# Attention and mixture of experts on one core: where the shared expert's tiles stand among the attention slots, and identity products in the slots without a tile

## The reference

```python
def _L0_attn_ref(x, Wq, Wk, Wv, norm_w, Wo, bo, diff_weight):
    ...
    scores = jnp.einsum('bqhif,bkhif->ibhqk', qs, ks_) * scale
    atts = jax.nn.softmax(scores, axis=-1)
    att = atts[0] - diff_weight * atts[1]
    o = jnp.einsum('bhqk,bkhe->bqhe', att, vs)
    rms = jax.lax.rsqrt(jnp.mean(o * o, axis=(-2, -1), keepdims=True) + eps)
    ...
def _L0_ffn_ref(x, Wg, Ws1, Ws3, Ws2, We1, We3, We2):
    gates = jax.nn.sigmoid(xf @ Wg)
    vals, idx = jax.lax.top_k(gates, TOP_K)                      # 2 of 8 experts
    ...
    shared = jax.nn.silu(xf @ Ws1) * (xf @ Ws3) @ Ws2            # every token
    h = jax.nn.silu(jnp.einsum('td,edf->tef', xf, We1)) * jnp.einsum('td,edf->tef', xf, We3)
    routed = jnp.einsum('tef,efd,te->td', h, We2, w)
    out = (shared + routed) / (N_SHARED + TOP_K)
...
xn = _layernorm(x, axis=-1)
x = x + _L0_attn_ref(xn, ...) + _L0_ffn_ref(xn, ...)
```

## Time and profile before

| what | value |
|---|---|
| median of 3 runs | 660.99 us (656.55 to 661.47) |
| the profiled execution | 660.85 us, span of its trace 658.8 us |
| PE busy (matmul) | 632.3 us, 96% of the span |
| DVE busy | 481.4 us, 73% |
| ACT busy | 413.4 us, 63% |
| mean granted TensorE clock | 0.916 |
| start of slot 0, slot 8, slot 40, slot 44, slot 116, slot 126 | 53.3, 96.1, 254.5, 273.5, 599.1, 638.3 us |

### The profile page before, as it was taken

How to read it: one execution, slowest core, us unless ns; L and a number is a source line. 1 busy time by engine, 2 the same in 40 slices (tenths; PEclk the granted TensorE clock), 3 DMA queues, 4 the chain that set the end, 5 groups by cost and what they waited for, 6 DMA issues and landing times.

```text
span 658.8 us, 13172 instructions
## 1 busy us (share of the span) xinstructions
PE 632.3 (96%) x4501; PEld 352.5 (53%) x4501; DVE 481.4 (73%) x1012; ACT 413.4 (63%) x808; POOL 219.5 (33%) x296
## 2 busy tenths in 40 slices
PE   7799999999999999999999999999999999999995
PEld 6445434545454344365666665656556656655553
DVE  4999667867786576677777787777777787776374
ACT  4543456655664556677777777777677766677662
POOL 5620053554454453022323232233323242333000
PEclk9667769987996679799999999999999999999998
DMA  6975202240141302547245734746344725220741
GB/s 171 204 135 115 72 28 48 62 98 22 35 93 31 88 26 82 125 129 209 87 150 129 216 105 132 182 137 188 120 109 121 233 80 172 81 71 17 209 134 49
DMA packets 62529, 74.04 MB, mean 112 GB/s; under 512 B 7296, under 2 KB 42496, under 8 KB 62464
## 3 DMA queue, kind: packets, MB, share of 16 engines
q1 hardware_dynamic: 57952, 64.00, 37.4%
q0 software_dynamic: 4352, 8.95, 4.0%
q10 hardware_dynamic: 160, 0.26, 0.2%
HBM read 40.08 MB, written 15.80 MB: 85 GB/s over the span
## 4 chain that ended last, share of the span: by engine, by line
PE 82%; DVE 7%; issue 5%; ACT 3%; POOL 1%; DMA 1%; SPq 0%; POOLq 0%; DVEq 0%; ACTq 0%
PE O L1114 19%; PE ST L1097 17%; PE F L1152 11%; PE F L1165 8%; PE ST L1102 7%; PE F L1149 4%; DVE rowmax L809 3%; PE S L1078 3%; PE F L1132 2%; PE F L1047 2%; ACT probs L626 1%; PE O L988 1%; PE F L1063 1%; PE F L1004 1%; PE F L1038 1%
## 5 line engine op out<-in xcount | busy, mean ns | idle before, releaser
L809 DVE TENSOR_REDUCE rowmax<-S 128x1 f32<-128x512 f32 x486 | 313.6, 684 | 94.2 <-PE S L1078 86.3
L626 ACT ACTIVATE probs<-ST 128x512 f32<-128x512 f32 x490 | 266.0, 595 | 144.5 <-PE ST L1102 131.1
L1097 PE MATMUL ST<-qop,kop 32*128 32x512 f32 x490 | 147.1, 521 | 6.1 <-ACT probs L626 4.9
L1078 PE MATMUL S<-kop,qop 32*128 32x512 f32 x486 | 147.1, 526 | 2.4 <-DMA kop<-kparts 0.9
L1114 PE MATMUL O<-probs,vop 128*32 128x512 f32 x1024 | 138.2, 652 | 0.0
L460 POOL DMA_INDIRECT yt<-ysb,xst x72 | 72.3, 1004 | 147.3 <-DMA yt<-ysb,xst 137.3
L1097 PEld LDWEIGHTS ST<-qop,kop 32*128 32x128 f32 x490 | 59.1, 190 | 111.5 <-ACT probs L626 73.7
L1102 PE MATMUL ST<-mop,ones_r 2*128 2x512 f32 x490 | 117.8, 433 | 0.0
L449 POOL DMA_INDIRECT xs<-xn,slot_i x64 | 62.9, 983 | 74.9 <-DVE rowmax L809 59.8
L1152 PEld LDWEIGHTS F<-xsT,wrt_all 128*128 128x128 f32 x576 | 69.7, 191 | 26.0 <-issue 26.0
L1152 PE MATMUL F<-xsT,wrt_all 128*128 128x128 f32 x576 | 83.4, 288 | 0.0
(11 more groups left out here) (154 smaller groups left out, 608.1 us busy)
## 6 DMA issues: line engine op xcount, KB each, us to landing
wrt_all<-in_wexp SPq DMA_DIRECT2D x72, 384.0 KB
qop<-qparts SPq DMA_DIRECT2D x64, 128.0 KB
kop<-kparts SPq DMA_DIRECT2D x62, 128.0 KB
xs<-xst SPq DMA_DIRECT2D x12, 387.0 KB, 6.5
xst<-xs SPq DMA_DIRECT2D x36, 129.0 KB
base<-in_x SPq DMA_DIRECT2D x8, 256.0 KB, 4.7
xn<-yt SPq DMA_DIRECT2D x8, 256.0 KB, 4.8
out_x<-base SPq DMA_DIRECT2D x7, 256.0 KB, 3.3
```

The lines of the kernel that those rows point to most:

```text
L626: A(probs[:, n % NP, :], st_bank(n)[:, :], ACT.Exp, scale=SCALE).then_inc(s_p, 1)
L809: V.reduce_max(rowmax[hf][:, (k + 2) % BANDS, q // QT % HC, q % QT:q % QT + 1], s_bank(n)[:, :], AX).then_inc(s_mx, 1)
L1078: mm(s_bank(n)[:, :], qop[b % 2][at:at + BAND, c, t * P:(t + 1) * P], kop[b % 2][at:at + BAND, c, :], start=True, stop=True, tile_position ...
L1097: mm(st_bank(n)[:, :], kop[b % 2][at:at + BAND, c, t * P:(t + 1) * P], qop[b % 2][at:at + BAND, c, :], start=True, stop=False, tile_positi ...
```

## The change

The 16 shared tiles now stand in every pair from slot 8 to slot 38, so that with the routed tiles all pairs from 8 to 114 have one. The bare pairs are still twelve: those that begin in slots 0, 2, 4, 6, 40, 42, 116, 118, 120, 122, 124 and 126. Every half of a slot of a bare pair gets identity products, 12 in slots 0 to 7 and 7 in the others, into F[0], in slots 4 and 5 into F[1] (the prefix sums of the routing use F[0] there). That is 192 + 56 + 168 = 416 of them; before there were 84 in the loop, six in each half of slots 115, 118, 119, 122, 123, 126 and 127.

```diff
-    SH_AT = [0, 2, 8, 10, 12, 14, 18, 20, 24, 26, 30, 34, 38, 116, 120, 124]
+    SH_AT = [8 + 2 * i for i in range(SH_TILES)]
...
+    def bare(slot):
+        return 0 <= slot < SLOTS and tile_at(slot - slot % 2) is None
...
-                    if k == 1 and RT_AT[-1] < slot < SLOTS and slot % 4 in (2, 3):
-                        keep_busy(6, 0)
+                    if k == 1 and bare(slot):
+                        keep_busy(12 if slot < 8 else 7, 1 if slot in (4, 5) else 0)
...
-                        if RT_AT[-1] < slot < SLOTS and slot % 4 in (2, 3):
-                            keep_busy(6, 0)
+                        if bare(slot):
+                            keep_busy(12 if slot < 8 else 7, 1 if slot in (4, 5) else 0)
```

## The result

The changed kernel takes 637.46 us (median of 4 runs, 636.86 to 639.11), the kernel before 660.92 (4 runs, 656.55 to 661.47). The ratio is 0.9651 with a 95% interval of 0.9601 to 0.9701: 3.5% faster. Forecast were 635 us and a range of 630 to 645.

The account below looks back on a forecast made before the run. TensorE's work and the clock it runs at were taken to bound the kernel. Terms -8.2 - 13.3 - 0.4 - 0.9 - 3.0 + 0.2 = -25.6 us gave 635 us, range 630 to 645.

Parts of the forecast that it names:

- the removed wait: Slot 115: twelve identity products go, with a 0.59 us wait for `gate_u`; -0.9 us for slots 44 to 115.
- Slots 8 to 39: All 16 pairs have a tile, ten plain ones at 8.8 us; 158.4 becomes 145.1 us, -13.3.
- Slots 0 to 7: First four pairs with 12 identity products a half; 42.8 becomes 34.6 us, -8.2, if the clock stays full.
- so the full clock is my value: Slots 0 to 7: full clock assumed from slot 118's six identity products a half; at the lower level 53 us, +10.
- the clock is lost once in slots 0 to 3: Rival: TensorE runs short during VectorE's reciprocal in slots 0 to 3; +1 to +6.5 us, about 641 us; chance 0.20.
- the clock holds: Forecast case: full clock with identity products in the bare pairs, 630 to 638.5 us; chance 0.62.
- Slots 116 to 125: Tiles leave these pairs and identity products enter the bare halves; 39.2 becomes 36.2 us, -3.0.
- Slots 40 to 43: Two bare pairs gain 28 identity products each, 0.9 us counted as hidden in waits; 19.0 becomes 18.6 us, -0.4.
- The remaining terms: Slots 44 to 115 at -0.9 us and slots 126 on at +0.2 us.
- Stretches of score products alone lose the clock, and products on all 128 rows keep it: Cause taken for clock falls behind bare pairs in slots 0 to 43; how few full-height products suffice was left open.
- only the cost: Rival: falls have another cause and come as often, so tiles and identity products only add time; 674 us; chance 0.03.
- VectorE becomes the bound: Rival: in slots 8 to 39 VectorE's share leaves little, 0.5 us of waits a pair; +8, 643 us; chance 0.06.

Follow-up runs that it names:

- the table alone: Kernel before with only the new placement of shared tiles (every pair from slot 8 to 38), identity products left as they were: 635.37 us, ratio 0.9751.
- the fillers alone: Changed kernel with the shared tiles put back in their old slots, so only the identity products in bare pairs are new: 642.42 us, ratio 0.9871.
- the short fillers: Changed kernel with the same number of identity products in the slots, each on 32 rows of the array instead of 128: 644.91 us, ratio 0.9907.
- the wait for mop filled: Changed kernel with 30 identity products in slot 0's second half, 7 in slots 2 to 7, behind slot 116 only 20, ending slot 119: 625.44 us.

## Why the prediction was right, and where not

**What bounds the kernel** was read rightly: TensorE's work and the clock it is granted. The gain came where the clock row had its sixes and sevens, and slots 44 to 115 changed by the 0.9 us that the removed wait was priced at.

**Slots 8 to 39** was the largest term (-13.3 forecast, -14.4 measured). The ten plain pairs were taken at 8.8 and came at 8.7. Both halves of the change give it: the table alone reached 147.1 with one fall on entering, the fillers alone 141.0 on the old table.

**Slots 0 to 7** is the term that was mis-sized: -8.2 forecast, -4.4 measured. The step that failed first is "so the full clock is my value". The nearest row had six fillers a half, but with weigh products between its groups; in slots 0 and 1 VectorE sets the pace and the groups stand 2.3 us apart once. The rival "the clock is lost once in slots 0 to 3" named this place and this reason and priced it at +1 to +6.5; it cost 2.3, for in the run with 30 fillers in that half slots 0 to 3 held 1.00 and took 17.6 instead of 19.9 us. The other 1.5 of the 3.8 us are a price: at 1.00 slots 0 to 3 took 17.6 against 16.8 forecast, and slots 4 to 7, at 1.00 in the changed kernel too, 18.5 against 17.8. That the total still came within the band of "the clock holds" (630 to 638.5) is in part luck: slots 8 to 39 and 40 to 43 were 1.9 us shorter than forecast and hid half of the miss.

**Slots 116 to 125** was right in size (-3.0, measured -3.1) and its working was incomplete. I priced the fillers as part of what the bare pairs must have. The runs without them took 27.7 us when the clock held and 35.4 to 37 when it did not, so the gain of 3.1 is made of 11.5 that go with the moved tiles and the old fillers, and 8.4 that the fillers of the change take. The table alone, with the old fillers, took 30.0 us here: the new ones made the stretch 6.1 us longer than it was without them.

**Slots 40 to 43** came at 17.8 instead of 18.6: more of the fillers were hidden in waits than I counted. Here too the runs without them are the other half of the account: 16.5 us where the clock held, 20.3 where it did not. The remaining terms were right to 0.1 us.

**The mechanism.** "Stretches of score products alone lose the clock, and products on all 128 rows keep it" is borne out by the fillers on the old table, by the short fillers in slots 6 and 7, and by the filled half of slot 0: all four traces with 30 fillers there and no tile hold 1.00 in slots 0 to 7, and all four that have 12 in every half lose it. For the filled wait in slot 119 it is likely and not shown. The rival "only the cost" is out: fillers alone made the kernel faster. "VectorE becomes the bound" is out as well: in slot 16's pair VectorE is busy 6.7 of 8.7 us. Whether a given bare pair loses the clock in a given execution stays open; the same file did both.

One reading of the prediction was wrong in a way that helps its cause. It says that a bare pair holds no full-height product in its second slot, and calls slot 22 an exception. But its transposes are on 128 rows too, and `weigh_at` puts both calls of `weigh` into the even slot only where that slot's number is divisible by four; in the others the second call stands in the odd slot. The kernel before in slot 16 (its second call and the start of slot 17, which has none), then in slot 23:

```profile
138.17 1.06 PE L1114 MATMUL O<-probs,vop 128*32 128x512 f32 x8
139.16 0.59 PE L1097 MATMUL ST<-qop,kop 32*128 32x512 f32 x2
...
168.98 0.96 PE L1097 MATMUL ST<-qop,kop 32*128 32x512 f32 x2
170.11 1.07 PE L1114 MATMUL O<-probs,vop 128*32 128x512 f32 x8
```

Behind slots 16, 28, 32, 36 and 40, which have no `weigh` in their second slot, the next pair lost the clock each time (mean 0.54, 0.62, 0.51, 0.84 and 0.66); behind slot 22, which has one, it did not. So slot 22 fits the cause better than the prediction knew. This is read from one trace, the table alone once kept the clock behind slot 40 all the same, and no run moved `weigh` alone.

## What to carry to other kernels

Read the granted clock by stretch before counting work: a matrix engine that is busy throughout can run at the lower level (14.6 us of 14.6 at 0.54 in slot 18 of the kernel before), and then it pays to have dense work in every stretch, real or filler. Put fillers first where the engine waits anyway (under the reciprocal of 1.74 us, in the 1.3 us for the DMA), where they cost next to nothing, and only then on the path, where they cost 8.4 us in the last slots. Compare several executions of such a kernel, since the same program falls in some and not in others, and a filler's worth is partly its effect on that spread.

## What was not expected of the hardware

The lower level can outlast dense work. In the kernel with 30 fillers in slot 0, a fall at 590.0 lasted 37.5 us with TensorE busy in 36.7 of them, weigh products on all rows in every slot; the clock came back at 627.5, near the end of the 28 identity products that stand behind slot 127. In slots 8 to 39 of the kernel before the clock came back within a pair or two each time. The clock row of the kernel with 30 fillers in slot 0, and then of the one with the wait for mop filled, show it in the last slices:

```profile
PEclk9769999999999999999999999999999999999557
```

```profile
PEclk9768999999999999999999999999999999999999
```

Without any filler of their own, slots 120 to 125 kept the full clock in the two traces in which it did not fall at this wait (27.7 us for slots 116 to 125); in the five with a fall they did not regain it. So the few us around one wait of 1.3 us decide over about 10 us. Why one execution gets through them and the next does not stays open.
